# A gated 256-step recurrence on one core: the gate by Sigmoid, an early visit to the loop's code, and another order of waits

## The chip, the cores and the metric

The kernel runs on one core of a Trainium2 chip. The metric is the device time of one execution in microseconds; before the change it is 207.98 us, the median of three runs (206.93 to 208.17).

## What is computed

The input x has 32 sequences (B) of 256 steps (T) with 256 features (D); cond has 256 features for each sequence. Two layers follow one another, each added to its input. The first is a Haar transform with a gate between analysis and synthesis. As the gate is the same for all levels, the transform and its inverse cancel, and the layer is a scaling:

```python
h    = silu(cond @ W1.T + b1)
gate = sigmoid(h @ W2.T + b2)          # (32, 256)
x    = x + (x + x * gate[:, None, :])  # = x * (2 + gate)
```

The second is a recurrence over the 256 steps with the state h, 32 x 256, which begins as cond:

```python
xW = x @ Wx + b
h  = tanh(h @ Wh + xW[:, t])           # for t = 0 .. 255
x[:, t] = x[:, t] + h
```

## The kernel before

The features lie on the partitions, in two halves of 128 (the index k for an input half, m for an output half); a step is 32 columns. Everything is fp32 but the bias, which is laid by bf16 products. x stays on the chip in x1, in 16 chunks of 16 steps. Steps are worked in turns of four (TURN), each turn in two parts of two steps (PART).

What sets the order is written out by hand, one program for each engine, with semaphores between them:

- TensorE (lines 173 to 277) runs a hardware loop of 64 turns (line 269). For each step s of a turn it first fills: it lays bias and input products of later steps into PSUM (`fill`, line 247; nothing at s = 0, then 24, 20 and 28 products), and then adds the products of Wh with the new state (`recur`, line 206), 16 of them. Every product of 128 x 128 weights is cut into four of 32 output features (`by_columns`, line 181), each with its own weight load; an fp32 product shows twice in the profile, a bf16 one once. bank_e holds half m = 0, bank_l half m = 1. The loop's first instruction stands at slot 0 of a block of 256 instruction slots (`head_slot`), and with its weight loads the body is some 500 instructions long, so it takes two such blocks.
- ScalarE (line 142) runs two tanh for each step, from PSUM into h_ring, which has four slots (lines 163 to 171). It waits for z_whole[m], the sum being complete. At even steps from 4 on it also waits for out_ready, that is for VectorE to have added the old states of these slots to the output; this wait is written ahead of the other:

```python
                if t >= TURN and t % 2 == 0:
                    act.wait_ge(out_ready, t // 2 - 1)
                for m in range(HALVES):
                    act.wait_ge(z_whole[m], t + 1)
                    nc.scalar.activation(h_ring[...], z_of(s, m), ACT.Tanh)
```

- VectorE (line 280) scales x by g_t = 2 + gate twice for each part: into x_ring for TensorE (input_ready) and in place (x1_ready); it adds the state (`add_out`, line 299).
- SP (line 120) loads and stores. GpSimd only clears b_parts.

Ahead of the loop stands the first stage. TensorE warms up with ten products of ones (line 210), then computes cond W1, keeps busy with `keep_warm`, then the product with W2, again `keep_warm`, then the recurrence's first step from cond with Wh, the bias and the first input products (lines 227 to 243). Between these ScalarE and VectorE make the gate from tanh alone: silu from tanh(z/2) and z (lines 154 to 157 and 313), the gate from tanh (line 160), then g_t = 0.5 tanh + 2.5 (line 325) and x times g_t (`scale_first`, line 294). b is brought in as three equal rows, from which VectorE makes three bf16 parts by two subtractions (lines 316 and 319). The loads leave on SP's queue in the order w1 (half 0), w2, the first two steps of x, Wx, Wh, the rest of x's first chunk (lines 121 to 126), and on ScalarE's: w1 (half 1), b (lines 144 to 146).

Of the kernel before, what the change touches and what calls it, by code (L numbers as in the profile page):

```python
# [10 lines left out]
P = 128  # L11
# [3 lines left out]
def build(nc, x, w1_cond, w2, wx, wh, b_rows, out):  # L15
# [12 lines left out]
    with ExitStack() as ctx:  # L28
# [12 lines left out]
        half_b = sb("half_b", [P, HALVES, 2])  # L41
        ones = sb("ones", [P, P], BF16)

        b_parts = sb("b_parts", [P, D])

        table_t = sb("table_t", [P, 1])
        z = sb("z", [P, HALVES, B])
        tanh_z = sb("tanh_z", [P, HALVES, B])  # L50
        tanh_z2 = sb("tanh_z2", [P, HALVES, B])
        silu2 = sb("silu2", [P, HALVES, B])
        g_t = sb("g_t", [P, HALVES, B])

# [17 lines left out]

        def high_half(tile):
            return tile.bitcast(BF16).rearrange("p (n two) -> p n two", two=2)[:, :, 1]
# [11 lines left out]
        x_first_loaded = sem("x_first_loaded")  # L86
        x_loaded = [sem(f"x_loaded_{c}") for c in range(CHUNKS)]
        ones_ready = sem("ones_ready")
        b_cleared = sem("b_cleared")
        b_ready = sem("b_ready")  # L90
        half_b_ready = sem("half_b_ready")
        z1_product = sem("z1_product")
        z2_product = sem("z2_product")
        z_ready = sem("z_ready")
        tanh_z1_ready = sem("tanh_z1_ready")
        tanh_z2_ready = sem("tanh_z2_ready")
# [18 lines left out]
        FIRST = PART * B  # L115
# [22 lines left out]
        @block.gpsimd  # L138
        def _(pool):
            nc.gpsimd.memset(b_parts[:], 0.0).then_inc(b_cleared, 1)  # L140

        @block.scalar
        def _(act):
            act.dma_start(w1_t[:, 1, :], w1_cond[:, 1, :]).then_inc(w1_loaded[1], DMA)
            act.wait_ge(b_cleared, 1)
            act.dma_start(b_parts[32:97:32, :], b_rows).then_inc(b_loaded, DMA)
# [3 lines left out]
            nc.scalar.activation(table_t[:], ones[:, 0:1], ACT.Tanh)  # L150
            act.wait_ge(half_b_ready, 1)
            for m in range(HALVES):
                act.wait_ge(z1_product, m + 1)
                nc.scalar.activation(tanh_z[:, m, :], z_ps[0][m], ACT.Tanh, bias=half_b[:, m, 0:1],
                                     scale=0.5).then_inc(tanh_z1_ready, 1)
                nc.scalar.activation(z[:, m, :], z_ps[0][m], ACT.Identity, bias=w1_t[:, m, D + B:D + B + 1])\
                    .then_inc(z_ready, 1)
            for m in range(HALVES):
                act.wait_ge(z2_product, m + 1)
                nc.scalar.activation(tanh_z2[:, m, :], z_ps[1][m], ACT.Tanh, bias=half_b[:, m, 1:2],  # L160
                                     scale=0.25).then_inc(tanh_z2_ready, 1)
# [12 lines left out]
        def _(pe):  # L174
            def warm_up(n):
                for _ in range(n):
                    nc.tensor.matmul(idle_ps, ones[:], ones[:, 0:1].to_broadcast([P, 256]), start=True, stop=True)  # L177
# [18 lines left out]
            def lay_bias(s, steps, m, opens=True):  # L196
                by_columns(z_of(s, m, steps), high_half(b_parts[:, m * P:(m + 1) * P]), ones[:, 0:steps * B],
                           start=opens)
# [7 lines left out]
            def recur(s, k, m, h, start=False):  # L206
                return by_columns(z_of(s, m), wh_sb[:, k, m * P:(m + 1) * P], h, start=start, stop=(k == HALVES - 1))

            pe.wait_ge(ones_ready, 1)
            warm_up(10)  # L210
            for m in range(HALVES):
# [7 lines left out]
            for k in range(HALVES):  # L219
                pe.wait_ge(silu_ready, k + 1)  # L220
                for m in range(HALVES):
                    done = gate_product(1, k, m, w2_t, silu2)
                    if k == HALVES - 1:
                        done.then_inc(z2_product, 1)
            keep_warm(3)

            pe.wait_ge(wh_loaded, DMA)
            for m in range(HALVES):
                for k in range(HALVES):
                    recur(0, k, m, cond_t[:, k, :], start=(k == 0))  # L230
            pe.wait_ge(b_ready, 2)
            lay_bias(0, 2, 0, opens=False)
            lay_bias(0, 1, 1, opens=False)
            lay_bias(1, 1, 1)
            pe.wait_ge(wx_loaded, DMA)
            for m in range(HALVES):
                for k in range(HALVES):
                    if m == 0:
                        pe.wait_ge(first_input_ready, k + 1)
                    done = lay_input(0, 1 if m else 2, k, m)  # L240
                done.then_inc(z_whole[m], 1)
# [27 lines left out]
            with nc.Fori(1, TURNS + 1, engines=bass.OrderedEngineSet([pe.engine]), head_slot={pe.engine: 0}) as turn:  # L269
# [10 lines left out]
        def _(dve):  # L280
# [3 lines left out]


            def scale(turn, part, in_place):
                c, cols = steps_of(turn, part)
                raw = x1[:, c, :, cols].rearrange("p k (s b) -> p k s b", b=B)
                ring = x_ring[:, :, part * PART * B:(part + 1) * PART * B].rearrange("p k (s b) -> p k s b", b=B)
                return nc.vector.tensor_tensor(raw if in_place else ring, raw,  # L290
# [15 lines left out]
            for k in range(HALVES):  # L306
                dve.wait_ge(w1_loaded[k], DMA)
            nc.vector.tensor_scalar(half_b[:], w1_t[:, :, D + B:], 0.5, None, ALU.mult)\  # L308
                .then_inc(half_b_ready, 1)
            for m in range(HALVES):  # L310
                dve.wait_ge(z_ready, m + 1)
                dve.wait_ge(tanh_z1_ready, m + 1)
                nc.vector.scalar_tensor_tensor(out=silu2[:, m, :], in0=tanh_z[:, m, :], scalar=1.0, in1=z[:, m, :],
                                               op0=ALU.add, op1=ALU.mult).then_inc(silu_ready, 1)
            dve.wait_ge(b_loaded, DMA)
            nc.vector.tensor_tensor(b_parts[64:97, :], b_parts[64:97, :], high_half(b_parts[64:97, :]), ALU.subtract)\
                .then_inc(b_ready, 1)
            dve.wait_ge(b_ready, 1)
# [3 lines left out]
            dve.wait_ge(x_first_loaded, DMA)  # L322
            for m in range(HALVES):
                dve.wait_ge(tanh_z2_ready, m + 1)
                nc.vector.tensor_scalar(g_t[:, m, :], tanh_z2[:, m, :], 0.5, 2.5, ALU.mult, ALU.add)\
                    .then_inc(g_ready, 1)
                dve.wait_ge(g_ready, m + 1)
                scale_first(m)
            dve.wait_ge(x_loaded[0], DMA)
            scale(0, 1, in_place=False).then_inc(input_ready[1], 1)  # L330
            dve.wait_ge(first_input_ready, HALVES)
            scale(0, 0, in_place=True).then_inc(x1_ready, 1)
            dve.wait_ge(input_ready[1], 1)
            scale(0, 1, in_place=True).then_inc(x1_ready, 1)

            for turn in range(TURNS):
# [5 lines left out]
                if more:  # L342
                    if (t + TURN) % CS == 0:
                        dve.wait_ge(x_loaded[(t + TURN) // CS], DMA)
                    scale(turn + 1, 0, in_place=False).then_inc(input_ready[0], 1)
                else:
                    nc.vector.memset(x_ring[:, :, 0:PART * B], 0.0).then_inc(input_ready[0], 1)
                dve.wait_ge(x1_ready, 2 * turn + 1)
# [53 lines left out]
```

## Time and profile before

| | |
|---|---|
| three runs | 207.98 us median, 206.93 to 208.17 |
| the profiled execution | 206.96 us |
| its span, first to last instruction | 205.1 us |
| TensorE busy (products; weight loads) | 181.2 us (88%); 165.3 us (81%) |
| VectorE; ScalarE busy | 97.3 us (47%); 76.7 us (37%) |
| mean granted TensorE clock | 1.000 |

The page's busy shares are averages over the span. "Idle before" in a timeline row is the time in which the engine did nothing ahead of that instruction, with what ended it; "issue" there means that it waited for nothing that the profile shows. "ACTq" in the chain is an entry of ScalarE's queue that only waits for a semaphore, with the line that wrote the wait.

### The profile page before, as it was taken

The numbers are of one execution on the slowest core, as the hardware profiler recorded it, in microseconds if no ns is written. First come the engines' busy times: TensorE is split into PE (matmuls) and PEld (weight loads), VectorE is DVE, ScalarE is ACT, GpSimd is POOL, SyncE is SP. The second block draws the span as 40 slices with busy tenths as digits, with TensorE's granted clock in tenths as the row PEclk, the third lists the DMA queues.
The fourth block names the chain that finished last, engine by engine and source line by source line (L and its number), as shares of the span: only waits on it lengthen the run. The fifth ranks groups of instructions, "written<-read, shape, count | busy, mean of one in ns | idle before, by whom it ended". The sixth has DMA issues, their size and how long they took to land.

```text
span 205.1 us, 33574 instructions
## 1 busy us (share of the span) xinstructions
PE 181.2 (88%) x16058; PEld 165.3 (81%) x16058; DVE 97.3 (47%) x395; ACT 76.7 (37%) x520; POOL 0.5 (0%) x5
## 2 busy tenths in 40 slices
PE   6678988988998898899889889988988988998895
PEld 3578888888888888888888888887888888888885
DVE  1435455454445545444554544454455454445543
ACT  4123333333333333333333333333333333333332
POOL 1000000000000000000000000000000000000000
PEclk9999999999999999999999999999999999999999
DMA  5409999402020020202002020200202020020212
GB/s 146 172 6 333 400 415 407 186 0 102 0 101 2 0 104 0 102 0 101 1 2 102 0 104 0 101 1 2 102 0 102 0 85 19 0 104 0 102 51 51
DMA packets 6962, 17.99 MB, mean 88 GB/s; under 512 B 1699, under 2 KB 2726, under 8 KB 6950
## 3 DMA queue, kind: packets, MB, share of 16 engines
q1 hardware_dynamic: 6800, 17.71, 23.2%
q10 hardware_dynamic: 150, 0.15, 0.2%
q14 instruction: 9, 0.07, 0.1%
q8 instruction: 3, 0.05, 0.1%
HBM read 9.48 MB, written 8.39 MB: 87 GB/s over the span
## 4 chain that ended last, share of the span: by engine, by line
PE 84%; ACT 6%; issue 4%; DMA 2%; SPq 1%; ACTq 1%
PE bank_e L183 48%; PE bank_l L183 36%; ACT h_ring L170 6%; DMA wh_sb<-in_wh 2%; ACTq L169 1%; SPq L124 0%; SPq L123 0%; SPq L122 0%; SPq L121 0%
## 5 line engine op out<-in xcount | busy, mean ns | idle before, releaser
L183 PE MATMUL bank_e<-h_ring,wh_sb 128*32 128x32 f32 x4096 | 103.5, 201 | 18.4 <-ACT h_ring L170 17.9
L183 PEld LDWEIGHTS bank_e<-h_ring,wh_sb 128*32 128x32 f32 x4096 | 76.0, 110 | 32.0 <-ACT h_ring L170 25.7
L183 PE MATMUL bank_l<-h_ring,wh_sb 128*32 128x32 f32 x4096 | 99.7, 197 | 0.0
L170 ACT ACTIVATE h_ring<-bank_e 128x32 f32<-128x32 f32 x256 | 50.5, 197 | 122.4 <-PE bank_e L183 111.7
L302 DVE TENSOR_TENSOR x<-x,h_ring 128x128 f32<-128x128 f32 x129 | 37.5, 291 | 95.6 <-ACT h_ring L170 95.6
L183 PE MATMUL bank_l<-x_ring,wx_sb 128*32 128x32 f32 x4128 | 79.6, 199 | 0.0
L183 PEld LDWEIGHTS bank_l<-h_ring,wh_sb 128*32 128x32 f32 x4096 | 77.6, 111 | 0.0
L183 PE MATMUL bank_e<-x_ring,wx_sb 128*32 128x64 f32 x2064 | 73.9, 228 | 0.0
L183 PEld LDWEIGHTS bank_l<-x_ring,wx_sb 128*32 128x32 f32 x4128 | 61.8, 111 | 0.0
L183 PE MATMUL bank_l<-ones,b_parts 128*32 128x32 bf16 x1032 | 54.1, 180 | 0.0
L170 ACT ACTIVATE h_ring<-bank_l 128x32 f32<-128x32 f32 x256 | 49.8, 194 | 0.2 <-issue 0.2
L183 PEld LDWEIGHTS bank_e<-x_ring,wx_sb 128*32 128x32 f32 x2064 | 44.9, 110 | 1.1 <-issue 1.1
L183 PEld LDWEIGHTS bank_l<-ones,b_parts 128*32 128x32 bf16 x1032 | 38.5, 98 | 0.0
L290 DVE TENSOR_TENSOR x<-x,g_t 128x128 f32<-128x128 f32 x128 | 36.8, 288 | 2.4 <-issue 0.2
L290 DVE TENSOR_TENSOR x_ring<-x,g_t 128x128 f32<-128x128 f32 x127 | 36.1, 284 | 3.0 <-DMA x<-in_x 1.7
L183 PE MATMUL bank_e<-ones,b_parts 128*32 128x64 bf16 x516 | 30.1, 195 | 0.9 <-issue 0.9
L183 PEld LDWEIGHTS bank_e<-ones,b_parts 128*32 128x32 bf16 x516 | 17.8, 98 | 0.0
L177 PE MATMUL bank_e<-ones 128*128 128x256 bf16 x10 | 2.3, 416 | 1.0 <-DVE ones L305 1.0
L177 PEld LDWEIGHTS bank_e<-ones 128*128 128x128 bf16 x10 | 1.3, 140 | 1.6 <-DVE ones L305 1.0
L150 ACT ACT_TABLE_LOAD x1 | 1.3, 1283 | 2.5 <-issue 2.5
L183 PEld LDWEIGHTS bank_e<-w_t,wh_sb 128*32 128x32 f32 x16 | 0.3, 148 | 1.6 <-DMA wh_sb<-in_wh 1.6
L308 DVE TENSOR_SCALAR half_b<-w_t 128x4 f32<-128x4 f32 x1 | 0.2, 169 | 2.9 <-DMA w_t<-in_w_cond 2.9
(25 smaller groups left out, 10.8 us busy)
## 6 DMA issues: line engine op xcount, KB each, us to landing
x<-in_x SPq DMA_DIRECT2D x15, 512.0 KB, 9.4
out_dram<-x SPq DMA_DIRECT2D x15, 512.0 KB, 3.4
x<-in_x SPq DMA_DIRECT2D x1, 448.0 KB, 5.5
w_t<-in_w SPq DMA_DIRECT2D x1, 256.0 KB, 3.3
wx_sb<-in_wx SPq DMA_DIRECT2D x1, 256.0 KB, 4.8
wh_sb<-in_wh SPq DMA_DIRECT2D x1, 256.0 KB, 4.8
out_dram<-x SPq DMA_DIRECT2D x1, 256.0 KB, 2.4
w_t<-in_w_cond SPq DMA_DIRECT2D x1, 145.0 KB, 2.9
```

What stands on the lines that cost most here:

```text
L150: nc.scalar.activation(table_t[:], ones[:, 0:1], ACT.Tanh)
L169: act.wait_ge(z_whole[m], t + 1)
L170: nc.scalar.activation(h_ring[:, m, s * B:(s + 1) * B], z_of(s, m), ACT.Tanh)\
L177: nc.tensor.matmul(idle_ps, ones[:], ones[:, 0:1].to_broadcast([P, 256]), start=True, stop=True)
L183: done = nc.tensor.matmul(out[q:q + 32], weights[:, q:q + 32], moving, start=start, stop=stop, skip_group_check=True)
L290: return nc.vector.tensor_tensor(raw if in_place else ring, raw, g_t[:].unsqueeze(2).to_broadcast([P, HALVES, PART, B]), ALU.mult)
L302: nc.vector.tensor_tensor(x1[:, c, :, cols], x1[:, c, :, cols], h_ring[:, :, s * B:(s + steps) * B], ALU.add).then_inc(out_ready, 1)
L308: nc.vector.tensor_scalar(half_b[:], w1_t[:, :, D + B:], 0.5, None, ALU.mult)\
```

## The change

What it does, in the order of the diff:

- x's first turn (four steps) comes as an array of its own, x_head, 1 KB for each partition, and is scaled from there. x1 gets the rest of the first chunk, which SP asks for once Wx has landed.
- ScalarE's queue issues w1 (half 1), x_head and Wh; b goes to GpSimd's queue, behind a memset that is now 512 columns wide.
- The gate uses Sigmoid with the bias in the activation: two activations in place of four for the first layer. VectorE makes silu straight from PSUM. The first scaling computes (gate + 2) * x in one operation; g_t is made later, once.
- b is held twice. The first use in steps 0 and 1 is one fp32 product with the whole b (the other two of its three rows are zero there); the three bf16 parts are needed only from the loop on, and VectorE makes them after the first scaling.
- TensorE branches after the warm-up to a small block placed just ahead of the loop, in the loop's block of instruction slots, runs one product of 32 columns there, and branches back. The loop's first instruction now stands at slot 6. Two keep_warm calls have fewer rounds (3 become 1 and 1).
- The order in which waits are written is turned round on ScalarE and at three places on VectorE, and some waits on VectorE go.

```diff
         def _(sp):
             sp.dma_start(w1_t[:, 0, :], w1_cond[:, 0, :]).then_inc(w1_loaded[0], DMA)
             sp.dma_start(w2_t[:], w2).then_inc(w2_loaded, DMA)
-            sp.dma_start(x1[:, 0, :, 0:FIRST], x[:, 0, :, 0:FIRST]).then_inc(x_first_loaded, DMA)
             sp.dma_start(wx_sb[:], wx).then_inc(wx_loaded, DMA)
-            sp.dma_start(wh_sb[:], wh).then_inc(wh_loaded, DMA)
+
+            sp.wait_ge(wx_loaded, DMA)
             sp.dma_start(x1[:, 0, :, FIRST:N], x[:, 0, :, FIRST:N]).then_inc(x_loaded[0], DMA)
...
         def _(pool):
-            nc.gpsimd.memset(b_parts[:], 0.0).then_inc(b_cleared, 1)
+            nc.gpsimd.memset(b_sb[:], 0.0).then_inc(b_cleared, 1)
+            pool.wait_ge(b_cleared, 1)
+            pool.dma_start(b_sb[32:97:32, :, :], b_rows).then_inc(b_loaded, DMA)
...
             act.dma_start(w1_t[:, 1, :], w1_cond[:, 1, :]).then_inc(w1_loaded[1], DMA)
-            act.wait_ge(b_cleared, 1)
-            act.dma_start(b_parts[32:97:32, :], b_rows).then_inc(b_loaded, DMA)
+            act.dma_start(x_head[:], x_first).then_inc(x_head_loaded, DMA)
+            act.dma_start(wh_sb[:], wh).then_inc(wh_loaded, DMA)
...
                 act.wait_ge(z1_product, m + 1)
-                nc.scalar.activation(tanh_z[:, m, :], z_ps[0][m], ACT.Tanh, bias=half_b[:, m, 0:1],
-                                     scale=0.5).then_inc(tanh_z1_ready, 1)
-                nc.scalar.activation(z[:, m, :], z_ps[0][m], ACT.Identity, bias=w1_t[:, m, D + B:D + B + 1])\
-                    .then_inc(z_ready, 1)
+                nc.scalar.activation(sig_z1[:, m, :], z_ps[0][m], ACT.Sigmoid, bias=gate_b(0, m))\
+                    .then_inc(sig_z1_ready, 1)
...
-                if t >= TURN and t % 2 == 0:
-                    act.wait_ge(out_ready, t // 2 - 1)
                 for m in range(HALVES):
                     act.wait_ge(z_whole[m], t + 1)
+
+                    if m == 0 and t >= TURN and t % 2 == 0:
+                        act.wait_ge(out_ready, t // 2 - 1)
...
             warm_up(10)
+            only_pe = bass.OrderedEngineSet([pe.engine])
+            nc.br("pe_visit", engines=only_pe)
+            stage = nc.switch_bb("pe_first_stage")
...
+            pe.addr_align(bass.FETCH_BLOCK_INSTRUCTIONS, offset=0, max_nops=0)
+            nc.br("pe_loop", engines=only_pe)
+            with nc.body("pe_visit", parent=stage.parent, valid_engines=only_pe):
+                warm_up(1, 32)
+                nc.br("pe_first_stage", engines=only_pe)
+            nc.switch_bb("pe_loop")
...
             def scale_first(k):
-                raw, ring = (a[:, k, 0:PART * B].rearrange("p (s b) -> p s b", b=B) for a in (x1[:, 0], x_ring))
-                nc.vector.tensor_tensor(ring, raw, g_t[:, k, :].unsqueeze(1).to_broadcast([P, PART, B]), ALU.mult)\
+                raw, ring = (a[:, k, 0:PART * B].rearrange("p (s b) -> p s b", b=B) for a in (x_head, x_ring))
+                factor = gate[:, k, :].unsqueeze(1).to_broadcast([P, PART, B])
+                nc.vector.scalar_tensor_tensor(out=ring, in0=factor, scalar=2.0, in1=raw, op0=ALU.add, op1=ALU.mult)\
                     .then_inc(first_input_ready, 1)
```

On ScalarE, in the recurrence: two tanh of step 3 (bank_e1, bank_l11) and the first ones of step 4, before. An instruction carries only the last of the waits in its bracket itself; the others are entries of their own ahead of it.

```order
L170 ACTIVATE h_ring<-bank_e1 128x32 [waits z_whole_0]
L170 ACTIVATE h_ring<-bank_l11 128x32 [waits z_whole_1]
L170 ACTIVATE h_ring<-bank_e0 128x32 [waits z_whole_0,out_ready]
L170 ACTIVATE h_ring<-bank_l00 128x32 [waits z_whole_1]
L170 ACTIVATE h_ring<-bank_e0 128x32 [waits z_whole_0]
```

And now:

```order
L176 ACTIVATE h_ring<-bank_e1 128x32 [waits z_whole_0]
L176 ACTIVATE h_ring<-bank_l11 128x32 [waits z_whole_1]
L176 ACTIVATE h_ring<-bank_e0 128x32 [waits out_ready,z_whole_0]
L176 ACTIVATE h_ring<-bank_l00 128x32 [waits z_whole_1]
L176 ACTIVATE h_ring<-bank_e0 128x32 [waits z_whole_0]
```

Nothing moved but the order inside the bracket of each even step's first tanh: z_whole is now what the instruction itself waits for.

On TensorE, from the warm-up (ones) to the first product of the gate (w1_t), before:

```order
L177 MATMUL bank_e1<-ones 128x256 [waits ones_ready]
L177 MATMUL bank_e1<-ones 128x256 x9
L183 MATMUL gate_bank_0<-w1_t 32x32 [waits w1_loaded_0]
L183 MATMUL gate_bank_0<-w1_t 32x32 x3
L183 MATMUL gate_bank_0<-w1_t 32x32 [waits w1_loaded_1]
```

And now:

```order
L183 MATMUL bank_e1<-ones 128x256 [waits ones_ready]
L183 MATMUL bank_e1<-ones 128x256 x9
L225 UNCONDITIONAL_BRANCH
L190 MATMUL gate_bank_0<-w1_t 32x32 [waits w1_loaded_0]
L190 MATMUL gate_bank_0<-w1_t 32x32 x3
L190 MATMUL gate_bank_0<-w1_t 32x32 [waits w1_loaded_1]
```

A branch stands between the warm-up and the gate's first product; it leads to the block in front of the loop.

On TensorE, between the gate's second product and the loop (wh_sb is Wh, wx_sb is Wx, x_ring the scaled input), before:

```order
L183 MATMUL bank_e1<-ones 32x256 x12
L183 MATMUL bank_e0<-w1_t,wh_sb 32x32 [waits wh_loaded]
L183 MATMUL bank_e0<-w1_t,wh_sb 32x32 x7
L183 MATMUL bank_l00<-w1_t,wh_sb 32x32 x8
L183 MATMUL bank_e0<-ones,b_parts 32x64 [waits b_ready]
L183 MATMUL bank_e0<-ones,b_parts 32x64 x3
L183 MATMUL bank_l00<-ones,b_parts 32x32 x4
L183 MATMUL bank_l01<-ones,b_parts 32x32 x4
L183 MATMUL bank_e0<-x_ring,wx_sb 32x64 [waits first_input_ready,wx_loaded]
L183 MATMUL bank_e0<-x_ring,wx_sb 32x64 x3
L183 MATMUL bank_e0<-x_ring,wx_sb 32x64 [waits first_input_ready]
L183 MATMUL bank_e0<-x_ring,wx_sb 32x64 x3
```

And now:

```order
L190 MATMUL bank_e1<-ones 32x256 x4
L190 MATMUL bank_e0<-one,b_sb 32x64 [waits one_ready,b_loaded]
L190 MATMUL bank_e0<-one,b_sb 32x64 x3
L190 MATMUL bank_l00<-one,b_sb 32x32 x4
L190 MATMUL bank_l01<-one,b_sb 32x32 x4
L190 MATMUL bank_e1<-ones 32x256 x4
L190 MATMUL bank_e0<-w1_t,wh_sb 32x32 [waits wh_loaded]
L190 MATMUL bank_e0<-w1_t,wh_sb 32x32 x3
L190 MATMUL bank_l00<-w1_t,wh_sb 32x32 x4
L190 MATMUL bank_e0<-w1_t,wh_sb 32x32 x4
L190 MATMUL bank_l00<-w1_t,wh_sb 32x32 x4
L190 MATMUL bank_e0<-x_ring,wx_sb 32x64 [waits first_input_ready,wx_loaded]
```

The bias comes first and in fp32 (`one`, `b_sb`), the wait for Wh moves behind it, eight of twelve keep_warm products of ones are left, in two groups, and the halves k are now the outer order.

## Rows read from the trace of the kernel before

**Rows 1.** The page, part 4: the chain that ended last, by engine.

```profile
PE 84%; ACT 6%; issue 4%; DMA 2%; SPq 1%; ACTq 1%
```

**Rows 2.** Timeline of ScalarE, 30 to 36 us: start us, us, what, idle before.

```profile
30.83 0.20 ACT L170 ACTIVATE h_ring<-bank_e 128x32 f32<-128x32 f32 x1 [0.49 <-PE bank_e L183]
...
31.55 0.20 ACT L170 ACTIVATE h_ring<-bank_e 128x32 f32<-128x32 f32 x1 [0.43 <-PE bank_e L183]
...
32.33 0.20 ACT L170 ACTIVATE h_ring<-bank_e 128x32 f32<-128x32 f32 x1 [0.49 <-PE bank_e L183]
```

**Rows 3.** The chain in order of time, a turn's end: start us, us, what.

```profile
20.06 0.02 ACTq L169
20.08 0.04 issue
20.12 0.21 ACT h_ring L170
```

**Rows 4.** The same chain, whole span: the same place of two turns, twelve apart.

```profile
33.96 0.38 PE bank_e L183 x17
...
69.89 0.38 PE bank_e L183 x17
```

**Rows 5.** Timeline, all engines, 10.3 to 11.5 and 24.2 to 24.9 us.

```profile
10.32 0.20 ACT L170 ACTIVATE h_ring<-bank_e 128x32 f32<-128x32 f32 x1 [0.99 <-PE bank_e L183]
...
11.11 0.32 PE L183 MATMUL bank_e<-h_ring,wh_sb 128*32 128x32 f32 x8
...
11.49 0.20 ACT L170 ACTIVATE h_ring<-bank_e 128x32 f32<-128x32 f32 x1 [0.87 <-PE bank_e L183]
...
24.24 0.26 PE L183 MATMUL bank_e<-h_ring,wh_sb 128*32 128x32 f32 x8
...
24.58 0.19 PEld L183 LDWEIGHTS bank_e<-x_ring,wx_sb 128*32 128x32 f32 x8
...
24.62 0.20 ACT L170 ACTIVATE h_ring<-bank_e 128x32 f32<-128x32 f32 x1 [0.49 <-PE bank_e L183]
...
24.87 0.16 PEld L183 LDWEIGHTS bank_e<-h_ring,wh_sb 128*32 128x32 f32 x8
```

**Rows 6.** Timeline, all engines, the first 9 us.

```profile
1.05 2.31 PE L177 MATMUL bank_e<-ones 128*128 128x256 bf16 x10 [1.05 <-DVE ones L305]
...
1.19 1.28 ACTq L146 DMA_DIRECT2D b_parts<-in_b_rows  x1
...
3.67 0.60 PEld L183 LDWEIGHTS gate_bank<-w_t 128*32 128x32 f32 x32 [0.79 <-DMA w_t<-in_w_cond]
...
4.85 0.30 ACT L156 ACTIVATE z<-gate_bank,w_t 128x32 f32<-128x32 f32 x1
...
5.18 0.19 DVE L313 SCALAR_TENSOR_TENSOR silu<-tanh_z,z 128x32 f32<-128x32 f32 x1 [0.16 <-ACT z L156]
...
5.41 0.42 DVE L316 TENSOR_TENSOR b_parts<-b_parts 33x256 f32<-33x256 f32 x1
...
5.83 0.46 ACT L160 ACTIVATE tanh_z<-bank_l,half_b 128x32 f32<-128x32 f32 x2 [0.68 <-PE bank_l L183]
...
7.64 0.31 PEld L183 LDWEIGHTS bank_e<-w_t,wh_sb 128*32 128x32 f32 x16 [1.61 <-DMA wh_sb<-in_wh]
...
8.92 0.20 ACT L170 ACTIVATE h_ring<-bank_e 128x32 f32<-128x32 f32 x1 [2.62 <-PE bank_e L183]
```

**Rows 7.** Timeline of TensorE: the two gaps that "issue" ended.

```profile
9.71 0.33 PE L183 MATMUL bank_e<-h_ring,wh_sb 128*32 128x32 f32 x8 [0.43 <-issue]
...
12.77 0.19 PE L183 MATMUL bank_e<-ones,b_parts 128*32 128x64 bf16 x1 [0.91 <-issue]
```

**Rows 8.** DMA by queue (packets, MB, share) at 7.2:7.3, 10.2:10.3 and 13.9:14.0 us.

```profile
q8 instruction: 1, 0.02, 62.2%
...
q8 instruction: 1, 0.02, 76.0%
...
q8 instruction: 1, 0.02, 59.1%
```

More of the change, by code:

```diff
@@ L40, in build @@
         wh_sb = sb("wh_sb", [P, HALVES, D])
-        half_b = sb("half_b", [P, HALVES, 2])
         ones = sb("ones", [P, P], BF16)
-        b_parts = sb("b_parts", [P, D])
+        one = sb("one", [P, 1])
+        b_sb = sb("b_sb", [P, 2, D])
+        b_parts, b_whole = b_sb[:, 0, :], b_sb[:, 1, :]
         table_t = sb("table_t", [P, 1])
[L49 to L52, printed above, removed]
+        sig_z1 = sb("sig_z1", [P, HALVES, B])
+        silu = sb("silu", [P, HALVES, B])
+        gate = sb("gate", [P, HALVES, B])
         g_t = sb("g_t", [P, HALVES, B])
+        x_head = sb("x_head", [P, HALVES, TURN * B])
         x1 = sb("x1", [P, CHUNKS, HALVES, N])
@@ L174, in _, with warm_up @@
         def _(pe):
-            def warm_up(n):
+            def warm_up(n, columns=256):
                 for _ in range(n):
-                    nc.tensor.matmul(idle_ps, ones[:], ones[:, 0:1].to_broadcast([P, 256]), start=True, stop=True)
+                    nc.tensor.matmul(idle_ps[:, 0:columns], ones[:], ones[:, 0:1].to_broadcast([P, columns]),
+                                     start=True, stop=True)
             def by_columns(out, weights, moving, start=False, stop=False):
@@ L221, in _ @@
                 for m in range(HALVES):
-                    done = gate_product(1, k, m, w2_t, silu2)
+                    done = gate_product(1, k, m, w2_t, silu)
                     if k == HALVES - 1:
                         done.then_inc(z2_product, 1)
-            keep_warm(3)
-            pe.wait_ge(wh_loaded, DMA)
[L228 to L234, printed above, removed]
+            keep_warm(1)
+            pe.wait_ge(b_loaded, DMA)
+            pe.wait_ge(one_ready, 1)
+            lay_whole_bias(0, 2, 0)
+            lay_whole_bias(0, 1, 1)
+            lay_whole_bias(1, 1, 1)
+            keep_warm(1)
+            pe.wait_ge(wh_loaded, DMA)
+            for k in range(HALVES):
+                for m in range(HALVES):
+                    recur(0, k, m, cond_t[:, k, :])
             pe.wait_ge(wx_loaded, DMA)
[L236 to L239, printed above, removed]
+            for k in range(HALVES):
+                pe.wait_ge(first_input_ready, k + 1)
+                for m in range(HALVES):
                     done = lay_input(0, 1 if m else 2, k, m)
-                done.then_inc(z_whole[m], 1)
+                    if k == HALVES - 1:
+                        done.then_inc(z_whole[m], 1)
             for k in range(HALVES):
@@ L266, in fill @@
                         lay_input(at, 1, 1, 1)
[L269 removed]
+            pe.addr_align(bass.FETCH_BLOCK_INSTRUCTIONS, offset=0, max_nops=0)
[4 more added lines that the diff above has]
+            nc.switch_bb("pe_loop")
+            with nc.Fori(1, TURNS + 1, engines=only_pe, head_slot={pe.engine: 6}) as turn:
                 for s in range(TURN):
@@ L305, in _ @@
             nc.vector.memset(ones[:], 1.0).then_inc(ones_ready, 1)
[L306 to L309, printed above, removed]
+            nc.vector.memset(one[:], 1.0).then_inc(one_ready, 1)
             for m in range(HALVES):
[L311 to L314, printed above, removed]
+                dve.wait_ge(sig_z1_ready, m + 1)
+                nc.vector.scalar_tensor_tensor(out=silu[:, m, :], in0=z_ps[0][m], scalar=gate_b(0, m),
+                                               in1=sig_z1[:, m, :], op0=ALU.add, op1=ALU.mult)\
+                    .then_inc(silu_ready, 1)
+            for m in range(HALVES):
+                dve.wait_ge(gate_ready, m + 1)
+                if m == 0:
+                    dve.wait_ge(x_head_loaded, DMA)
+                scale_first(m)
             dve.wait_ge(b_loaded, DMA)
@@ L317, in _ @@
                 .then_inc(b_ready, 1)
+            nc.vector.tensor_scalar(g_t[:], gate[:], 2.0, None, ALU.add).then_inc(g_ready, 1)
             dve.wait_ge(b_ready, 1)
@@ L320, in _ @@
                 .then_inc(b_ready, 1)
[L322 to L329, printed above, removed]
+            dve.wait_ge(g_ready, 1)
             scale(0, 1, in_place=False).then_inc(input_ready[1], 1)
-            dve.wait_ge(first_input_ready, HALVES)
             scale(0, 0, in_place=True).then_inc(x1_ready, 1)
-            dve.wait_ge(input_ready[1], 1)
             scale(0, 1, in_place=True).then_inc(x1_ready, 1)
```

53 lines of the change are left out of this document (30 added, 23 removed).

## The prediction

> **What bounds the kernel now.** I read the chain of waits first, then ScalarE's timeline in a steady turn, then the chain in detail at one turn's end, then the first 13 us on all engines, then the instruction fetches. The chain [rows 1] is TensorE for 84% and ScalarE for 6%, but that share hides the structure: the recurrence is a round trip, TensorE (32 fp32 products of a step) to ScalarE (tanh) and back, 256 times, and all input and bias products are fitted into the gaps. A turn (4 steps) takes 35.93 / 12 = 2.994 us [rows 4]; 64 of them are 191.6 of the 205.1 us span. So what counts is the length of a step, and then whatever lies ahead of the first turn.
>
> Two things stand out. First, the steps are not equal: the tanh starts are 0.72 us apart from an even step to the next odd one and 0.78 from odd to even [rows 2]; ScalarE is idle 0.49 us ahead of the even ones and 0.43 ahead of the odd. The chain shows why [rows 3]: at an even step a separate ScalarE queue entry of line 169 (the wait for z_whole, "ACTq L169") stands between the product and the tanh. Rows 5 give the control: step 2 has no wait for out_ready yet, and its tanh starts 11.49 - (11.11 + 0.32) = 0.06 us after its last product; step 18 has it, and starts 24.62 - (24.24 + 0.26) = 0.12 us after. An activation carries one wait itself, the other becomes an entry of its own.
>
> Second, the start: the first tanh of the recurrence is at 8.92 us [rows 6], then TensorE stands 0.43 us at the loop's entry and 0.91 us in the middle of its first turn, with "issue" as the cause, thus waiting for nothing of the program [rows 7]. Each of these ends about 2.5 us after one instruction packet of 0.02 MB begins (7.2 to 9.7; 10.2 to 12.8) [rows 7, 8]. The third packet begins 1.2 us after TensorE goes past 12.77, so I take a block of code to cost 1.2 + 2.45 = 3.65 us from asking to running. After the first turn no such gap comes back.
>
> **The change part by part.** (a) ScalarE's two waits change places. The order listing shows the instruction's own wait (last in the bracket) to be z_whole now, and out_ready the separate entry, which is satisfied long before (what it asks for is an addition of two steps before) and is passed while ScalarE waits anyway. Saved: 0.78 - 0.72 = 0.06 us at each even step from 4 on, 126 of them: 7.5 us. It lies on the path if TensorE keeps up. The products behind an odd tanh follow the filling without a gap (TensorE's 0.72 us: a step's products and 24 or 28 filling ones); those behind an even one wait for it, since the filling's last weight loads end at 24.58 + 0.19 = 24.77 and the next begins at 24.87 [rows 5]. 0.06 fits into these 0.10 us, so TensorE does not take over at once. Bounds: nothing, if the parity has another cause; 0.02 + 0.02 (the queue entry and half of the issue behind it) x 126 = 5.0 [rows 3]; at most 0.065 x 126 = 8.2. I take 7.5, the value of rows 2 and 5. VectorE's waits swap in the same way but it idles; only at the last step does it count, 0.05 us.
>
> (b) TensorE's visit. After the warm-up (first instruction at 1.05) it branches to the loop's block, which is not there: 3.65 us from about 1.3, so the first gate product, at 3.67 before [rows 6], starts near 4.95. The cover is the wait for w1, and 1.3 us stick out. The bounds are nothing (if the block is already on the way) and, if the code behind is dropped, a rival below. The block after it is asked for on arrival, ready by 4.95 + 3.65 = 8.6. In return the 0.43 and 0.91 us of rows 7 go. Of the 0.43 I count 0.33, as the step's second tanh, 0.1 us behind that of 8.92 by the spacing of a pair, ends inside it.
>
> (c) The gate. ScalarE's four activations, the last at 4.85 [rows 6] and some 0.17 apart, become two, and the second silu needs neither the identity nor its place in the row: 2 x 0.17 = 0.35 us less in the 5.18 - 3.67 = 1.51 us from first product to second silu [rows 6]. So second silu at 4.95 + 1.16 = 6.1; the gate's activation 0.65 later as before (5.83 - 5.18), at 6.75. Then g_t no longer stands ahead of the first scaling, 2 x 0.19 us less (it is of the size of a silu): the sigmoids end at 7.03 and 7.2, the first inputs are ready near 7.3 and 7.5.
>
> (d) TensorE behind the gate. Wh was the last thing waited for (1.61 us, to 7.64), behind x's first columns and Wx on one queue. It now leaves as ScalarE's third DMA instead of SP's fifth, some 1.1 us earlier (an issue takes about 0.45), with the rest of x held back until Wx is in: I expect it by 6.5, hidden behind the gate. From there TensorE itself is late: free at 6.6, it has the work that took 8.92 - 7.64 = 1.28 us, plus 12 more product halves for the fp32 bias (0.2) and two short warm-ups (0.2 each, ten take 2.31 in rows 6), 1.9 in all: first tanh at 8.5 to 8.6, a gain of 0.35 us.
>
> (e) b goes from ScalarE's queue to GpSimd's, behind a memset twice as large. Before, it was in at 5.41 at the latest, 4.2 us after its issue began at 1.19 [rows 6]. Issued at 1.4 it is in at 5.6; needed at 6.8, it has 1.2 us of cover, and beyond that each microsecond costs one. The Trainium skill (DMA: Bandwidth & Descriptors, Latency and other measured facts) gives a GpSimd-issued DMA a first byte about 0.4 us later than the other queues; with it, an estimate, b is in at 6.0 and the sum is the same. No trace of before has such a DMA.
>
> (f) The other half of x's first turn is now scaled after b's two subtractions (0.42 us each) on VectorE: ready near 8.8, when TensorE wants it. Nothing to 0.2 us. The rest of x is needed only a step later and lands near 9, as before.
>
> (g) Pace. By durations TensorE runs slower until 12.77: the same eight products take 0.32 us at 11.11 and 0.26 at 24.24, and a step 11.49 - 10.32 = 1.17 us instead of 0.72 to 0.78 [rows 2, 5]. With the loop earlier, about one more step falls into the slow stretch, and the idle during the visit may postpone its end: -0.3 us, from +0.3 to -1.3 (three steps).
>
> Start: 0.35 + 0.33 + 0.9 - 0.3 = 1.3 us; from -0.5 to 2.4. Whole: 7.5 + 1.3 + 0.05 = 8.85 us. The profiled execution took 206.96 (span 205.1 and 1.86 around it), at the low end of 206.93 to 208.17 with median 207.98; from it I get 198.1, from the median 199.1. I take the middle, 207.5 - 8.9 = 198.6 us.
>
> **The rivals.** R1: the separate wait costs nothing and parity is something else. For it: the even tanhs are those that come behind the longer fillings of 24 and 28 products. Against: step 2 is even, comes behind such a filling and lacks the 0.06 [rows 5]. Then only the start counts: 207.5 - 1.35 = 206.1.
>
> R2: the visit pushes out the code it left. Line by line TensorE then pays 3.65 us for the loop's block (to 4.95), for its own first block again (8.6), its second (12.25), the loop's (15.9) and the next (19.55, where 12.77 stood before): +6.8 us against -7.5, so 206.8. Against it: with a fetch of a further block at 13.9, behind the loop's two, the loop turns back without a gap, so at least three blocks are held [rows 8]; whether four are, no row says. The Trainium skill states such a rule (Runtime: NRT & Kernel Launch, Instruction fetch mechanics: a taken branch out of the current two-page window makes a fetch that execution waits for). By its two pages the loop and the fetched third could not stand together, and the trace has them so; for the first jump, rule and trace agree.
>
> R3, slower than before: with four of the twelve keep_warm products behind the gate gone and TensorE idle from 3.4 to 4.95, the slow pace holds on into the loop. Place: the first turns. Price: 1.17 - 0.75 = 0.42 us a step. It decides from 8.9 / 0.42 = 21 further slow steps, about 25 us; at 40 steps the time is 207.5 - 8.9 + 17 = 215.6. Against: the slow loop leaves TensorE hardly any idle, and before it sped up within two steps of steady work.
>
> **How the numbers follow.** The forecast 0.82, R1 0.07, R2 0.07, R3 0.02, something not listed 0.02. A measurement tells about 1% (2.1 us) from no change. R1 and R2 are within it unless something adds; of them I count 0.04 as faster with part of (a). Faster 0.88, same 0.09, slower 0.03. Range: low end 206.9 - 8.2 - 2.4 = 196.3; high end 208 with the low bound of (a), 5.0, and a start that gains 0.5: 202.5. Its own range and that of the whole are nearly one, 196.3 to 202.5.
>
> **What would show it.** In the profile after: all tanh starts 0.72 us apart and no "ACTq" in the chain ((a); a turn of 2.88 us). TensorE's gate products near 4.95 and one instruction packet near 2.5 us, another near 6 (b). No "issue" gap at the loop's entry or in its first turn. First tanh of the recurrence at 8.5. Wrong would be: starts still 0.72 and 0.78 apart (R1); instruction packets one after another up to 19 us (R2); 0.32 us groups of products beyond 20 us (R3).

## The result, and the profile after

The changed kernel takes 197.86 us (median of 4 runs, 197.64 to 198.18) against 207.75 us (206.93 to 208.17) beside it: ratio 0.953, 95% interval 0.9496 to 0.9564. Its profiled execution took 198.18 us with a span of 196.4, against 206.96 and 205.1 before: 8.7 us less span.

The page of the changed kernel, part 4, against [rows 1]:

```profile
PE 88%; ACT 7%; issue 4%; DVE 0%
```

SP's and ScalarE's queues, 1% each before, are gone, and so is the DMA's 2%. Now ScalarE's timeline in a steady turn, against [rows 2] (start us, us, what, idle before):

```profile
30.80 0.20 ACT L176 ACTIVATE h_ring<-bank_e 128x32 f32<-128x32 f32 x1 [0.43 <-PE bank_e L190]
...
31.52 0.20 ACT L176 ACTIVATE h_ring<-bank_e 128x32 f32<-128x32 f32 x1 [0.43 <-PE bank_e L190]
...
32.24 0.20 ACT L176 ACTIVATE h_ring<-bank_e 128x32 f32<-128x32 f32 x1 [0.43 <-PE bank_e L190]
```

All steps are 0.72 us apart; the 0.78 of every second one is gone. The chain shows where it went. At the end of a turn, where [rows 3] has an "ACTq" entry, it now has only the first two lines below. The other two are the same place of two turns, twelve apart, as in [rows 4]:

```profile
22.16 0.02 issue
22.18 0.20 ACT h_ring L176
...
35.31 0.32 PE bank_e L190 x17
...
69.79 0.32 PE bank_e L190 x17
```

(69.79 - 35.31) / 12 = 2.873 us against 2.994. Over 63 turns that is 7.6 of the 8.7 us less span.

The start is the part that came out otherwise. The timeline of all engines, against [rows 6] and [rows 7]:

```profile
1.55 0.63 POOL L149 DMA_DIRECT2D b_sb<-in_b_rows  x1 [0.29 <-POOL b_sb L147]
...
5.85 0.21 PE L183 MATMUL bank_e<-ones 128*128 128x32 bf16 x1 [2.48 <-issue]
6.10 0.52 PEld L190 LDWEIGHTS gate_bank<-w_t 128*32 128x32 f32 x32
...
6.93 0.47 DVE L340 SCALAR_TENSOR_TENSOR silu<-gate_bank,w_t,sig_z 128x32 f32<-128x32 f32 x2 [5.92 <-ACT sig_z L162]
...
7.93 0.47 ACT L166 ACTIVATE gate<-bank_l,w_t 128x32 f32<-128x32 f32 x2 [0.82 <-PE bank_l L190]
...
8.39 0.42 PEld L190 LDWEIGHTS bank_e<-w_t,wh_sb 128*32 128x32 f32 x8
...
9.85 0.20 ACT L176 ACTIVATE h_ring<-bank_e 128x32 f32<-128x32 f32 x1 [1.45 <-PE bank_e L190]
...
10.47 0.34 PE L190 MATMUL bank_e<-h_ring,wh_sb 128*32 128x32 f32 x8 [0.36 <-ACT h_ring L176]
...
11.09 0.20 ACT L176 ACTIVATE h_ring<-bank_e 128x32 f32<-128x32 f32 x1 [0.93 <-PE bank_e L190]
...
12.10 0.20 ACT L176 ACTIVATE h_ring<-bank_e 128x32 f32<-128x32 f32 x1 [0.71 <-PE bank_e L190]
```

The visited product runs at 5.85 us, so the gate's first product comes at 6.10 instead of 3.67, and the first tanh at 9.85 instead of 8.92. At the loop's entry 0.36 us are still lost; the 0.91 us gap in the first turn is gone. The fifth tanh after and before:

```profile
13.54 0.20 ACT L176 ACTIVATE h_ring<-bank_e 128x32 f32<-128x32 f32 x1 [0.43 <-PE bank_e L190]
```

```profile
14.14 0.20 ACT L170 ACTIVATE h_ring<-bank_e 128x32 f32<-128x32 f32 x1 [0.49 <-PE bank_e L183]
```

The start has gained 0.60 us in all. It is made up of 0.93 us lost at the first tanh, 0.07 gained at the entry, 0.91 gained in the turn, and 0.55 gained because TensorE works at its faster pace earlier.

The 7.6 and 0.6 us leave 0.5. That is two long steps of the old profile which the new one does not have. One, ahead of the tanh at 27.05 us, is 0.2 us too long; the other, 0.3 us, is this one in the chain of before:

```profile
141.60 0.32 issue
```

Instruction packets come at 3.4, 6.8 and 13.0 us, and no others; from the DMA by queue, 3.4 to 3.5 us (packets, MB, share):

```profile
q8 instruction: 1, 0.02, 60.4%
q1 hardware_dynamic: 10, 0.02, 52.5%
```

The page's DMA issues and those of the first 15 us (KB, us from issue to landing):

```profile
wx_sb<-in_wx SPq DMA_DIRECT2D x1, 256.0 KB, 5.7
wh_sb<-in_wh ACTq DMA_DIRECT2D x1, 256.0 KB, 5.9
...
b_sb<-in_b_rows POOLq DMA_DIRECT2D x1, 6.0 KB, 5.5
```

Wh landed at 7.57 us (1.67 + 5.9), and b, 5.5 us after its issue at 1.55, at 7.05.

### The profile page after: what moved, and what is told of

It reads as the page before. It is cut to its first block, busy times and chain, and to the rows that moved or that the text cites. A ratio compares the mean times of both kernels' runs of the same rounds, so it can differ in the third digit from the quotient of the medians.

```text
span 196.4 us, 33590 instructions
## 1 busy us (share of the span) xinstructions
PE 176.6 (90%) x16067; PEld 165.3 (84%) x16067; DVE 96.8 (49%) x394; ACT 76.9 (39%) x518; POOL 1.4 (1%) x6
## 3 DMA queue, kind: packets, MB, share of 16 engines
HBM read 9.48 MB, written 8.39 MB: 91 GB/s over the span
## 4 chain that ended last, share of the span: by engine, by line
PE 88%; ACT 7%; issue 4%; DVE 0%
PE bank_e L190 48%; PE bank_l L190 39%; ACT h_ring L176 7%; PE bank_e L183 1%; PE gate_bank L190 0%; ACT sig_z L162 0%; DVE silu L340 0%; DVE ones L336 0%
## 5 line engine op out<-in xcount | busy, mean ns | idle before, releaser
L190 PE MATMUL bank_l<-ones,b_sb 128*32 128x32 bf16 x1024 | 53.9, 180 | 0.0
L176 ACT ACTIVATE h_ring<-bank_l 128x32 f32<-128x32 f32 x256 | 50.5, 197 | 0.0
L190 PEld LDWEIGHTS bank_l<-ones,b_sb 128*32 128x32 bf16 x1024 | 38.2, 97 | 0.0
L320 DVE TENSOR_TENSOR x<-x,g_t 128x128 f32<-128x128 f32 x126 | 36.3, 288 | 2.2
L190 PE MATMUL bank_e<-ones,b_sb 128*32 128x64 bf16 x512 | 29.7, 195 | 0.0
L190 PEld LDWEIGHTS bank_e<-ones,b_sb 128*32 128x32 bf16 x512 | 17.7, 97 | 0.0
L183 PE MATMUL bank_e<-ones 128*128 128x256 bf16 (+1 forms) x11 | 2.5, 399 | 3.5 <-issue 2.5
L340 DVE SCALAR_TENSOR_TENSOR silu<-gate_bank,w_t,sig_z 128x32 f32<-128x32 f32 x2 | 0.5, 250 | 5.9 <-ACT sig_z L162 5.9
L162 ACT ACTIVATE sig_z<-gate_bank,w_t 128x32 f32<-128x32 f32 x2 | 0.5, 287 | 3.0 <-PE gate_bank L190 3.0
```

The costliest lines, as they stand in the source:

```text
L162: nc.scalar.activation(sig_z1[:, m, :], z_ps[0][m], ACT.Sigmoid, bias=gate_b(0, m))\
L183: nc.tensor.matmul(idle_ps[:, 0:columns], ones[:], ones[:, 0:1].to_broadcast([P, columns]), start=True, stop=True)
L190: done = nc.tensor.matmul(out[q:q + 32], weights[:, q:q + 32], moving, start=start, stop=stop, skip_group_check=True)
L320: return nc.vector.tensor_tensor(own if in_place else by_steps(x_ring[:, :, of_turn]), raw, g_t[:].unsqueeze(2).to_broadcast([P, HALVES, P ...
L340: nc.vector.scalar_tensor_tensor(out=silu[:, m, :], in0=z_ps[0][m], scalar=gate_b(0, m), in1=sig_z1[:, m, :], op0=ALU.add, op1=ALU.mult)\
```

## The experiments

Each time is a median. The kernel before stood beside each batch: 208.13 us (batch 1), 208.31 (2), 207.98 (3).

**Batch 1: what is the visit worth?** First the changed kernel again, as the control.

> The changed kernel unchanged, as the standard of this batch. Every theory: 197.9 us, within 0.3; first tanh of the recurrence at 9.85 us, a turn 2.87 us.

Measured: 197.94 us (197.37 to 198.41), ratio 0.9512 (0.9474 to 0.955); span 196.2, first tanh 9.91, entry gap 0.36. The start repeats.

Then without the visit:

```diff
-            nc.br("pe_visit", engines=only_pe)
-            stage = nc.switch_bb("pe_first_stage")
...
-            pe.addr_align(bass.FETCH_BLOCK_INSTRUCTIONS, offset=0, max_nops=0)
-            nc.br("pe_loop", engines=only_pe)
-            with nc.body("pe_visit", parent=stage.parent, valid_engines=only_pe):
-                warm_up(1, 32)
...
-            with nc.Fori(1, TURNS + 1, engines=only_pe, head_slot={pe.engine: 6}) as turn:
+            with nc.Fori(1, TURNS + 1, engines=only_pe, head_slot={pe.engine: 0}) as turn:
```

> The changed kernel without TensorE's early visit (the loop's head at slot 0 as before). Theory A, the visit costs about as much as it saves: the first gate product is back at 3.7 us instead of 6.1, but Wh lands only near 7.57 (issued 1.67 + 5.9), so the first tanh comes at 8.9, 0.95 us earlier, and the gap in the middle of the first turn, 0.9 us, is back: 197.9, within 0.4. The gap at the loop's entry is 0.36 to 0.43 in either kernel (it is not the fetch). Theory B, the visit saves both gaps, 1.3 us, and costs nothing: 199.2. Theory C, the visit is a loss: its 2.4 us come back whole: 196.5.

Measured: 200.53 us (199.51 to 202.44), ratio 0.966 (0.9611 to 0.9709): 2.6 us slower than the control. TensorE in this kernel:

```profile
3.61 0.74 PE L190 MATMUL gate_bank<-w_t 128*32 128x32 f32 x32 [0.23 <-DMA w_t<-in_w_cond]
...
6.26 0.44 PE L190 MATMUL bank_e<-one,b_sb 128*32 128x64 f32 x8 [0.47 <-DMA b_sb<-in_b_rows]
...
10.14 0.34 PE L190 MATMUL bank_e<-h_ring,wh_sb 128*32 128x32 f32 x8 [1.74 <-issue]
...
13.09 0.21 PE L190 MATMUL bank_e<-ones,b_sb 128*32 128x64 bf16 x1 [0.81 <-issue]
```

The first tanh is 1.8 us earlier (8.15), and all of it is lost at the two gaps, 2.55 us together; packets stand at 7.3 and 10.7 us. None of the three theories has this: even B, the dearest, said 199.2, and the entry gap is 1.74 us, not 0.36 to 0.43. In the four profiles without the visit and with products cut in four (before, e2, f1, g4) the loop's first product comes at 9.6 to 10.1 us, though the first tanh lies anywhere from 8.15 to 8.92. Without the visit the first tanh says nothing: code sets the second.

Two kernels made the visit earlier. The first goes before the warm-up and leaves the warm-up out (its ten products compute nothing), the second after two products of it:

```diff
-            warm_up(10)
+            warm_up(2)
```

> The visit stands ahead of the warm-up, which is left out (ten products of ones; only the one in the visited block remains). Theory T1, TensorE's sequencer reaches the branch late because the ten warm-up products stand ahead of it: the instruction packet begins at 2.1 us instead of 3.4, the gate's first product comes at 4.8 instead of 6.1, then Wh's landing at 7.57 bounds the first tanh at 8.9: 0.9 us saved, 197.0, if the slow pace ends when it did; each further slow step adds 0.4. Theory T2, the packet queues behind the data loads: it still begins near 3.4 us, the gate's first product at 6.1, 197.9.

> Two warm-up products ahead of the visit in place of ten. T1: the packet begins 0.21 us later than in the run with the visit first for each product, near 2.5 us, the gate's first product at 5.2, the time 197.0 to 197.4. T2: the packet begins at 3.4 as with ten, 197.9.

The diff is that of the second; the first has no `warm_up(10)` line at all. Measured: 198.28 us (197.87 to 198.8) and 198.15 us (197.61 to 198.65), ratios 0.9528 and 0.9519, both the control's. The packet came at 3.3 and 3.7 us and the visited product at 5.69 and 6.18, as if the branch had been where it was: an earlier request brings no earlier code.

**Batch 2: the parts alone.** The swap of ScalarE's two waits put into the kernel before, and taken out of the changed one:

```diff
-                if t >= TURN and t % 2 == 0:
-                    act.wait_ge(out_ready, t // 2 - 1)
                 for m in range(HALVES):
                     act.wait_ge(z_whole[m], t + 1)
+                    if m == 0 and t >= TURN and t % 2 == 0:
+                        act.wait_ge(out_ready, t // 2 - 1)
```

> The kernel before, with ScalarE's two waits of the even steps written the other way round and nothing else. Theory W (the entry of its own costs 0.06 us at 126 steps): 7.5 us less than before, 200.2 against 207.75, all tanh starts 0.72 us apart, a turn of 2.875 us. Rival (the parity has another cause): no change, 207.7.

> The changed kernel with ScalarE's waits in the old order. Theory W: 7.5 us more than the changed one, 205.4; steps 0.72 and 0.78 us in turn. Rival: 197.9.

Measured: the swap alone 200.26 us (198.84 to 201.2), ratio 0.9607 (0.953 to 0.9684), thus 8.05 us less, with 6.6 to 9.8 us in the interval; the changed kernel without it 206.15 us (205.71 to 206.32), 8.2 us more than the control of batch 1 and 7.9 by the ratios to the kernel before of each batch (0.9892 and 0.9512). The swap alone also has its tanh 0.72 us apart:

```profile
30.74 0.20 ACT L170 ACTIVATE h_ring<-bank_e 128x32 f32<-128x32 f32 x1 [0.43 <-PE bank_e L183]
31.46 0.20 ACT L170 ACTIVATE h_ring<-bank_e 128x32 f32<-128x32 f32 x1 [0.43 <-PE bank_e L183]
32.18 0.20 ACT L170 ACTIVATE h_ring<-bank_e 128x32 f32<-128x32 f32 x1 [0.43 <-PE bank_e L183]
```

ScalarE's timeline with the swap undone has the old rhythm back, in an otherwise new kernel:

```profile
30.20 0.20 ACT L175 ACTIVATE h_ring<-bank_e 128x32 f32<-128x32 f32 x1 [0.49 <-PE bank_e L189]
30.91 0.20 ACT L175 ACTIVATE h_ring<-bank_e 128x32 f32<-128x32 f32 x1 [0.43 <-PE bank_e L189]
31.69 0.20 ACT L175 ACTIVATE h_ring<-bank_e 128x32 f32<-128x32 f32 x1 [0.49 <-PE bank_e L189]
```

Its chain also has a stall like that of before, and the page an "ACTq 1%":

```profile
180.00 0.34 issue
```

The visit alone, put into the kernel before (branch, block and slot 6, as the diff above read backwards, but with a product of 256 columns):

> The kernel before with the visit alone (its product has 256 columns). The gate's first product moves from 3.67 to 6.1 us; the kernel's longer gate then ends at 9.5, behind Wh (7.6), the first tanh is near 10.6 instead of 8.9; the gap in the middle of the first turn (0.9) goes, that at the entry stays. Theory A: 207.75 + 1.7 - 0.9 = 208.5. Theory B (both gaps go, the visit is covered): 206.4.

Measured: 206.63 us (205.94 to 207.53), ratio 0.9914 (0.9885 to 0.9943), 1.7 us less. Its TensorE:

```profile
5.80 0.40 PE L177 MATMUL bank_e<-ones 128*128 128x256 bf16 x1 [2.43 <-issue]
...
10.87 0.27 PE L183 MATMUL bank_e<-h_ring,wh_sb 128*32 128x32 f32 x8 [0.47 <-issue]
```

The first tanh is at 10.04, 1.1 us later than before, and still the kernel gains. The gap at the entry has not closed; that in the turn has. The time is that of theory B, but not for its reason.

The changed kernel without its two keep_warm groups (products whose results nobody reads):

> The changed kernel without the two groups of four keep_warm products behind the gate. If TensorE's own queue sets the first tanh there, it comes 0.4 us earlier, at 9.45, and the time is 197.5 if the slow pace ends when it did (11.85 us). If these products are what ends the slow pace, it ends later, each slow step costs 0.4 us more, and the time is 197.9 to 199.

Measured: 197.92 us (197.59 to 198.23), ratio 0.9509 (0.9451 to 0.9567). The first tanh is 0.3 us earlier (9.56), the median the same. The slow pace did not last longer without these products: the loop's products run at the faster pace from the first one on.

**Batch 3: why does the visited code come at 5.85?** All loads wait until the visited product has run, so that nothing else moves while the code is fetched:

```diff
+            sp.wait_ge(visited, 1)
...
+            pool.wait_ge(visited, 1)
...
+            act.wait_ge(visited, 1)
...
-                warm_up(1, 32)
+                warm_up(1, 32).then_inc(visited, 1)
```

> The changed kernel with every load held back until TensorE's visit is over. Theory T2 (the instruction packet queues behind the data loads): it begins 1.2 us after the branch, at 2.2 to 2.5 us instead of 3.4 to 3.8, and the visited product starts near 4.7 instead of 5.85. Theory T3 (a jump to code that is not there takes this long by itself): the packet begins at 3.4 and the product starts at 5.85 as before. The whole is slower by the loads' delay either way, 4 to 5 us.

Measured (one run): 200.6 us, as the loads are late; that is 2.7 us above the control, where 4 to 5 were expected. But the packet and the product:

```profile
q8 instruction: 1, 0.02, 65.1%
```

```profile
4.52 0.21 PE L187 MATMUL bank_e<-ones 128*128 128x32 bf16 x1 [1.15 <-issue]
```

The packet is at 2.0 us instead of 3.4 and the product at 4.52 instead of 5.85. From packet to product it is 2.4 to 2.5 us in both. So the 1.4 us are waiting of the packet while the data loads are issued and moved.

Could the visit be had for less? With the first stage's products on whole 128 column weights (a quarter of the instructions) its code should be resident on return; with and without the visit:

```diff
-                return by_columns(z_ps[layer][m], w_t[:, k, m * P:(m + 1) * P], operand[:, k, :],
-                                  start=(k == 0), stop=(k == HALVES - 1))
+                return nc.tensor.matmul(z_ps[layer][m], w_t[:, k, m * P:(m + 1) * P], operand[:, k, :],
+                                        start=(k == 0), stop=(k == HALVES - 1), skip_group_check=True)
```

> The changed kernel with every product ahead of the loop whole (128 output columns) instead of in four, so that the first stage takes some 140 instructions instead of 400 and ends inside TensorE's first block; the loop then stands in the second and third. Theory L (the second block is there from the start, since no kernel here fetched it in the trace): the visit finds it and costs 0.3 us, the third block is fetched meanwhile; the gate's first product is at 3.7 to 4.0, Wh's landing at 7.5 bounds the first tanh at 8.5 or earlier, no gap in the first turn: 1.3 us less than the changed kernel, 196.6. Rival (the second block is fetched only once TensorE is in it or jumps to it): gap of 2.5 us at the visit as now, 197.9.

> The same without the visit. Theory L: the loop's entry costs its 0.36 us only, but the third block is asked for at the entry, so the gap in the middle of the first turn is there, 0.9 to 1.7 us: 197.5 to 198.3, 1 to 1.7 us more than with the visit, and half to one us more spread than with it. Rival: a gap of over 1 us at the entry too, 200.

Measured: 203.3 us (202.95 to 203.73) with and 202.9 us (202.31 to 203.42) without, both over 5 us slower than the control. The weight loads with the visit:

```profile
4.04 1.78 PEld L199 LDWEIGHTS gate_bank<-w_t 128*128 128x128 f32 x8 [0.93 <-DMA w_t<-in_w_cond]
```

About the visit, theory L is right: TensorE went to its second block and back without a gap; the one packet near it, at 3.5 us, begins when the visited product has run. The gate's first product is 0.27 us later than without the visit (4.04 against 3.77), but both waited for w1, which landed 3.25 us after its issue against 2.99, so this is no price of the visit. The gap that L expected in the first turn without the visit is not there: its packet comes at 11.7 us, ahead of the loop. The visit thus had nothing to save.

The total is missed by 5 to 7 us, as the price of whole weights was not in the expectation. 8 whole fp32 loads take 1.78 us where 32 loads of a quarter took 0.52, and the first tanh is at 13.65, 3.8 us later than in the changed kernel. Behind it the slow pace lasts to 19.6 us, with the visit too, which costs another 1.8 us by the eighth tanh (21.27 against 15.72):

```profile
19.29 0.31 PE L190 MATMUL bank_l<-h_ring,wh_sb 128*32 128x32 f32 x8
...
20.10 0.24 PE L190 MATMUL bank_e<-h_ring,wh_sb 128*32 128x32 f32 x8
```

Last, a second profile of the kernel without the visit:

> A second look at the changed kernel without the visit, whose times spread over 2.9 us. If the gaps at the fetches and the end of the slow pace make the spread, they differ from the first look (entry 1.74 us, middle 0.81, slow pace up to 13.9 us) by as much as the time does from 199.5.

Measured (one run): 200.24 us, span 198.5. Its TensorE and three of ScalarE's tanh:

```profile
9.59 0.33 PE L190 MATMUL bank_e<-h_ring,wh_sb 128*32 128x32 f32 x8 [0.98 <-issue]
...
13.02 0.21 PE L190 MATMUL bank_e<-ones,b_sb 128*32 128x64 bf16 x1 [1.29 <-issue]
```

```profile
15.89 0.20 ACT L176 ACTIVATE h_ring<-bank_e 128x32 f32<-128x32 f32 x1 [0.56 <-PE bank_e L190]
...
17.06 0.20 ACT L176 ACTIVATE h_ring<-bank_e 128x32 f32<-128x32 f32 x1 [0.87 <-PE bank_e L190]
17.78 0.20 ACT L176 ACTIVATE h_ring<-bank_e 128x32 f32<-128x32 f32 x1 [0.41 <-PE bank_e L190]
```

These are the sixth to eighth; the eighth is at 15.52 in the control. The same kernel as in batch 1 has other gaps (0.98 and 1.29, not 1.74 and 0.81), and its slow pace lasts to 17.1 us, not 14.0. Its eighth tanh is 0.87 us later than in batch 1 (17.78 against 16.91) and its time 0.73 us longer than that profile's 199.51, as expected if the start makes the spread.

## Why the prediction was right, and where it was not

The forecast was 198.6 us in 196.3 to 202.5; measured were 197.86. The total holds because its largest term does. The terms of the start were wrong in size and partly in kind, and that their sum fits is partly luck. In the profiled pair the start gave 0.6 us, not 1.3, and 0.5 us of long steps that no term covers made up for it. Over the medians the change is 9.9 us, of which (a) is some 8.1 and the start 1.8.

**(a), the wait order, right.** 7.5 us were taken. In the profiles the steady turns give 7.6; by runs it is 8.05 (swap alone) and 8.2 (swap undone), each way round alone. R1 falls with either. The runs don't tell 8.05 from 7.6, but the profiles have more than 7.6 as well: those of the old wait order (before, f2, f3) have two long steps each in the steady part, 0.5 us together, and none of the eleven others has one. Why the old order brings them is not shown.

**(b), the visit, mis-sized in three places.** The first step that failed is the visit's price, 3.65 us from about 1.3, by which the gate's first product starts near 4.95. That price was read between 10.2 and 13.9 us, with a quiet DMA. g1 shows that behind the loads the packet comes 1.4 us later, and e3 and e4 that asking earlier doesn't help. The gate came at 6.10 and the whole stage with it, so that the first tanh was at 9.85, not 8.5.

The second is that the 0.43 us of [rows 7] goes. 0.36 to 0.52 us stay at the entry in all eight profiles with the visit and products cut in four (the changed kernel, e1, e3, e4, f2, f3, f4, g1), where no packet is under way that could end them. So the entry costs this by itself where TensorE has nothing left to do: with whole weights (g2, g3) its older products run on beyond the first two tanh, and no gap shows. What in the entry takes this time is not shown. In the kernel before, the code seems to have come at about the same time as the entry was done. Where it comes later the gap is 0.98, 1.10 or 1.74 us (g4, f1, e2), and it ends 2.5 to 2.8 us after a packet begins.

The third is (g), that about one more step falls into the slow stretch: it has the wrong sign. With the visit and products cut in four, the last group of eight products at 0.32 us ends by 11.9 us (e3), by 11.1 (the changed kernel), or lies ahead of the loop (f3, f4, e4, g1). Without it the pace lasts to 11.5 us at least and 12.8 at most (before), and to 14.0 (e2), 16.1 (f1) and 17.1 (g4). What ends it is not shown, and the visit alone does not: g2 has one and keeps the pace to 19.6. So the visit costs more than predicted at the first tanh and gives back more behind it: 2.6 us (e2 against e1) and 1.7 us (f3 against before).

Of these, the start explains all in the profiled pairs of e2 and g4 against e1: the eighth tanh is 1.4 and 2.3 us later, the time 1.5 and 2.3 us longer. For f3 against before, the eighth tanh gives 0.6 us and the profiled times 0.7. The other 1.0 us of the medians is not in these two profiles: that of before, 206.96, is of one of its fastest executions. A start that varies also fits the spread, as 200.53 ranges over 2.9 us and the control over 1.0, but of the kernel without the visit only two executions were profiled (e2, g4).

**(c), the gate, right.** From the first product to the gate's activation it is 7.93 - 6.10 = 1.83 us against 2.16: 0.33 less, 0.35 predicted.

**(d), (e), the loads, mis-sized but harmless.** Wh was in at 7.57, not 6.5, and wanted only at 8.39. b was in at 7.05, not 5.6 to 6.0, and wanted at 7.75. In the changed kernel both are covered because the visit makes the gate late. Without it TensorE waited 0.47 us for b (e2), so the cover of 1.2 us had been used up. The Trainium skill (DMA: Bandwidth & Descriptors, Latency and other measured facts) gives a DMA issued by GpSimd a first byte about 0.4 us later. Here its landing took at least 1.3 us more than the 4.2 of [rows 6], beside other loads than before, so this is no clean measurement of the issuer.

**What (c) to (f) are worth together** depends on the visit. Without it: 200.26 (f1) and 200.53 (e2), no gain, since the first tanh is 0.3 us earlier but code sets the second. With it, and with the old waits in both, the kernels of one batch differ by these parts alone: 206.63 (f3) and 206.15 (f2), 0.5 us less. The ranges overlap, 205.94 to 207.53 and 205.71 to 206.32, so this is small at best. The product of the ratios says the same: swap and visit alone make 0.9607 x 0.9914 = 0.952, the whole change 0.953.

**R2** is refuted: the whole start has three packets, and none at the return to the first block, behind which the gate's product starts 0.25 us after the visited one. The prediction adds that for the first jump, rule and trace agree. No row of before shows a jump out of the code that is held; the changed kernel has one, and there a packet did come and TensorE stood until 5.85 us. g2 shows a jump to the next block that needs no packet. **R3** falls with the steps of 0.72 us from the third on.

No kernel tried beats the changed one; f4 equals it with less code.

## What to carry to other kernels

Where an engine waits for two semaphores and the round trip bounds the kernel, write the wait that ends last so that the instruction itself carries it: the other order cost 0.06 us at each of 126 steps and some long steps besides, 4% of this kernel for two moved lines. Before putting a fetch earlier, look at what is on the DMA queues at that time, and take the gain at the step where both versions run steadily, not at the first result: with the visit alone (f3) the first tanh moved by +1.1 us and the time by -1.7. And shortening a stage in front of a fetch that is late anyway gives nothing until the fetch goes too.

## What the runs showed of the hardware that was not expected

- An instruction packet of 0.02 MB starts at 2.0 us with idle queues (g1) and at 3.3 to 3.8 us among the loads. In both cases execution follows 2.4 to 2.5 us after it.
- TensorE's second block of code is there from the start: a visit to it and back needs no packet (g2). The third has to be fetched.
- TensorE's entry into the loop costs 0.36 to 0.52 us with its code present, but nothing where older products still run (g2, g3).
- TensorE has a slow pace, 0.32 us for eight products instead of 0.26. It ended ahead of the loop in some executions and at 19.6 us in another, and in two executions of one kernel it differs by 3.1 us. The views print a granted clock of 1.00 through it. But the traces hold clock records in seven of the profiles only, and the first of these begins at 12.0 us (before), 13.9 (e2), 11.4 (f2), 10.7 (f3), 9.8 (f4), 9.9 (e4) and 12.9 (g1): where the slow pace ends, as far as the products tell. Ahead of it, 1.00 means that there is no record. Among the other runs a mean granted clock below 1 (0.975 to 0.992) is found only in kernels without the visit (before, e2, f1). So the slow pace may be the lower level of the clock; no row shows it at that level, and it stays open.
- With whole fp32 weights of 128 columns TensorE makes one load in 1.78 / 8 = 0.22 us; cut in four, the same 128 columns take 4 x 0.52 / 32 = 0.065 us. Both are from the first stage.
- The DMA of 6 KB from GpSimd needed 5.5 us from issue to landing, about as long as those of 256 KB beside it.
